# The quantised linear layer (F2) set into the last head of the third attention layer (L2)

## The reference, cut to what matters

```python
x = x + tanh(g_xattn[2]) * L2_xattn(layernorm(x), ctx, Wq, Wk, Wv, Wo)   # 32 query heads of 128, 4 key/value heads
x = x + tanh(g_ffn[2]) * L2_ffn(layernorm(x), kernel, bias)
# L2_ffn: xq = fake_quant(x, 8 bit, per row); kq = fake_quant(kernel, 8 bit, per column)
#         y = xq @ kq + fake_quant(bias, 16 bit);  out = fake_quant(y, 8 bit, per row)
```

## Time and profile before

| | us |
|---|---|
| median of 3 runs | 1754.78 (1753.35 to 1755.42) |
| the profiled execution | 1753.51 |
| its span, first to last instruction | 1751.2 |
| granted TensorE clock over the span | 0.952 |
| PE busy | 1569.3 (90%) |
| DVE busy | 908.8 (52%) |
| ACT busy | 702.3 (40%) |
| POOL busy | 630.3 (36%) |

### The profile page before, as it was taken

One profiled execution on the slowest core, in us unless ns is written; L12 is line 12 of the kernel. 1 busy time (PEld: TensorE's weight loads), 2 busy tenths in 40 slices (PEclk: granted clock), 3 DMA queues, 4 the chain that ended last, 5 costly groups with the idle time before them and its releaser, 6 DMA issues. The chain is left out here.

```text
span 1751.2 us, 25554 instructions
## 1 busy us (share of the span) xinstructions
PE 1569.3 (90%) x8786; PEld 1236.8 (71%) x8786; DVE 908.8 (52%) x1777; ACT 702.3 (40%) x2015; POOL 630.3 (36%) x594
## 2 busy tenths in 40 slices
PE   5897979858889999999999998686899999999976
PEld 4565756547668888888888887565677777777752
DVE  4785558867531212221222223596776676667552
ACT  3442154344335444443543534452333333343321
POOL 3543145466223221331331312133644444444310
PEclk9998999978989999999999999896999999999996
DMA  5001010011221010110101000332212121211001
GB/s 199 1 1 48 25 42 13 1 65 59 67 67 48 13 49 1 61 49 2 49 5 44 25 25 1 126 73 73 73 49 73 49 85 43 79 49 49 13 16 48
DMA packets 27885, 81.41 MB, mean 46 GB/s; under 512 B 3248, under 2 KB 11952, under 8 KB 22768
## 3 DMA queue, kind: packets, MB, share of 16 engines
q1 hardware_dynamic: 26896, 79.44, 13.8%
q10 hardware_dynamic: 864, 0.30, 0.1%
HBM read 69.25 MB, written 10.49 MB: 46 GB/s over the span
## 5 line engine op out<-in xcount | busy, mean ns | idle before, releaser
L385 PE MATMUL bank<-hid_high,wq_high 128*128 128x512 f32 (+1 forms) x640 | 257.6, 403 | 6.8 <-issue 6.5
L385 PE MATMUL bank<-hid_high,wq_low 128*128 128x512 f32 (+1 forms) x640 | 239.5, 374 | 0.0
L385 PE MATMUL bank<-hid_low,wq_high 128*128 128x512 f32 (+1 forms) x640 | 238.1, 372 | 0.0
L1132 DVE SCALAR_TENSOR_TENSOR x_stream<-bank,gates,x_stream 128x512 f32<-128x512 f32 x64 | 48.1, 751 | 364.8 <-PE bank L1218 364.8
L982 POOL TENSOR_TENSOR probs_middle<-probs_middle,small 128x512 f32<-128x512 f32 x64 | 66.5, 1040 | 365.1 <-DVE small L1120 365.1
L1468 ACT ACTIVATE probs_last<-probs_last,small 128x64 f32<-128x64 f32 x256 | 86.0, 337 | 154.3 <-DVE small L1540 154.3
L385 PEld LDWEIGHTS bank<-hid_high,wq_high 128*128 128x128 f32 x640 | 122.4, 191 | 30.8 <-issue 9.8
L385 PEld LDWEIGHTS bank<-hid_high,wq_low 128*128 128x128 f32 x640 | 122.1, 191 | 23.0
L385 PEld LDWEIGHTS bank<-hid_low,wq_high 128*128 128x128 f32 x640 | 122.8, 192 | 21.0 <-issue 3.5
L1052 ACT ACTIVATE probs_middle<-pair,small 128x128 f32<-128x128 f32 x256 | 90.5, 366 | 75.5 <-DVE small L1114 75.5
L583 POOL TENSOR_TENSOR probs_first<-probs_first,small 128x512 f32<-128x512 f32 x64 | 66.7, 1043 | 134.2 <-DVE small L737 134.1
(11 more groups left out here) (277 smaller groups left out, 4010.5 us busy)
## 6 DMA issues: line engine op xcount, KB each, us to landing
raw_q<-in_L_wq SPq DMA_DIRECT2D x18, 1024.0 KB, 4.9
raw_o<-in_L_wo SPq DMA_DIRECT2D x18, 1024.0 KB, 4.8
values_last<-ctx_values SPq DMA_DIRECT2D x32, 256.0 KB, 3.9
values_t_last<-ctx_keys SPq DMA_DIRECT2D x8, 512.0 KB, 3.3
raw_c<-in_L_wkv SPq DMA_DIRECT2D x6, 512.0 KB, 3.7
x_stream<-in_x SPq DMA_DIRECT2D x8, 256.0 KB, 9.5
ctx_keys<-raw_o SPq DMA_DIRECT2D x8, 256.0 KB, 2.0
ctx_values<-raw_o SPq DMA_DIRECT2D x16, 128.0 KB, 2.4
```

The costliest lines, as they stand in the source:

```text
L385: last = k.nc.tensor.matmul(out, stationary(a, c), moving(b, c), start=n == 0, stop=n == total - 1)
L1132: nc.vector.scalar_tensor_tensor(xt, k.bank[7][:], gate, xt, ALU.mult, ALU.add).then_inc(k.x_done, 1)
```

## The change

F2 has no stage of its own. Its work is handed out by `linear_gpsimd`, `linear_scalar`, `linear_vector`, `linear_tensor` and called from attention_middle's last head. `F2_AT` is 13: linear step f stands in slot 13+f, so steps 0 to 5 run in slots 13 to 18, the rest behind the slots.
- Weights: greatest values on DVE at the end of slot 6, rounding on ACT at the end of slot 7, clipping on DVE at the end of slot 8, transposes on PE at the end of slots 11 and 12, evictions on ACT at the start of slots 12 and 13, the scales matmul at the end of PE's slot 13.
- The rounded weights are put in `raw_c`, where the bias goes too: its DMA waits for the scales matmul, and `fake_bias` follows in DVE's step 0.
- The rows of statistics are now taken for one tile at a time (`tile_stats`, then a power on POOL).
- On PE, transposes_x(t) stands in slot 15+t ahead of the attention's transposes and project; linear(t) at the slot's end. Both products use one bank each (4 and 5) instead of two.
- The sixteen context groups all stand behind the slots, four in each of tiles 4 to 7. The first unit's weights are split by ACT after its step 5 and by POOL ahead of its step 6.
- L3's first weights are fetched earlier. The scratch buffers are allocated once; L2's second query buffer is made of halves of `values_t` and `probs_t`.

```diff
@@ attention_middle, ACT @@
                 for s in range(SLOTS + (LAG if last else 0)):
+                    if last and s in (12, 13):
+                        integer_weights(2 * s - 24)
+                        integer_weights(2 * s - 23)
+                    if last and s == 14:
+                        weight_scales()
                     if lives(first, last, s):
                         exp(j, s)
+                    if last and s >= F2_AT + 2:
+                        integers(s - F2_AT - 2)
...
+                    if last and s == 7:
+                        round_weights(k.at("loaded_q", 32 * HEADS + 16))
+                    if last and s >= F2_AT:
+                        linear_step(s - F2_AT)
             heads(act, body)
+            for f in range(SLOTS + LAG - F2_AT, LIN_STEPS):
+                t = f - 2
+                if t < T:
+                    integers(t)
+                linear_step(f)
+                if t == 3:
+                    context_weights(0)
+                if 4 <= t < T:
+                    for g in range(4 * t, 4 * t + 4):
+                        context_evict(g)
+                if t == 4:
+                    context_weights(1)
@@ attention_middle, DVE @@
                     if lives(first, last, s - LAG):
                         out_low(j, s - LAG)
+                    if last and s == 6:
+                        weight_scales(k.at("loaded_q", 32 * HEADS + 16))
+                    if last and s == 8:
+                        clip_weights()
+                    if last and s == F2_AT - 1:
+                        tile_stats(0, updated + 1)
+                    if last and s >= F2_AT:
+                        linear_step(s - F2_AT, updated)
@@ attention_middle, PE @@
                     if lives(first, last, s):
                         scores(j, s)
+                    if last and s >= F2_AT + 2:
+                        transposes_x(s - F2_AT - 2)
...
                     if lives(first, last, s - LAG):
                         attend(j, s - LAG)
+                    if last and s in (11, 12):
+                        pe.wait_ge(k.q_sbuf, tile("q_sbuf", j, SLOTS))
+                        integer_weights(2 * s - 22)
+                        integer_weights(2 * s - 21)
+                    if last and s == 13:
+                        weight_scales()
+                    if last and s >= F2_AT + 2:
+                        linear(s - F2_AT - 2)
             heads(pe, body)
+            pe.wait_ge(k.exp_done, k.at("exp_done", SLOTS * HEADS))
+            for t in range(SLOTS + LAG_Y - F2_AT - 2, T):
+                transposes_x(t)
+                context_group(4 * t)
+                context_group(4 * t + 1)
+                linear(t)
+                context_group(4 * t + 2)
+                context_group(4 * t + 3)
@@ attention_middle, POOL @@
+                    if last and s >= F2_AT - 1:
+                        linear_step(s - F2_AT)
...
+            for f in range(SLOTS + LAG_Y - F2_AT, LIN_STEPS):
+                if f in (SLOTS + LAG_Y - F2_AT, SLOTS + LAG_Y - F2_AT + 1):
+                    context_weights(f - SLOTS - LAG_Y + F2_AT)
+                linear_step(f)
@@ linear_sync @@
+    fetch_ahead(k, sp, "L3", "q", k.wround_done, k.at("wround_done", C))
+    fetch_ahead(k, sp, "L3", "o", k.lo_o, used_o)
+    sp.wait_ge(k.wint_psum, k.at("wint_psum", C))
+    sp.wait_ge(k.scales_psum, k.at("scales_psum", 1))
+    sp.dma_start(m["bias"], k.args["F2_bias"].partition_broadcast(P)).then_inc(k.loaded_const, 16)
+    sp.wait_ge(k.s_psum, scores_done)
+    ctx_fetch(k, sp, 2, m["RAW"][0])
+    sp.wait_ge(k.o_psum, attend_done)
+    ctx_fetch(k, sp, 3, m["RAW"][1])
@@ linear_gpsimd, step(f) @@
+        if 0 <= f + 1 < T:
+            rstd(f + 1)
+        if 2 <= f < T + 2:
+            add_bias(f - 2)
@@ linear_scalar, step(f) @@
+        if f >= 4:
+            integers_y(f - 4)
+        if 1 <= f <= T:
+            round_x(f - 1)
+        if 3 <= f < T + 3:
+            round_y(f - 3)
@@ linear_vector, step(f, updated): order of the calls @@
+        normalise(f); fake_bias() at f == 0
+        greatest(f - 1); greatest_y(f - 3); scale, zero_to_one, inverse of both
+        update(f - 4); gated_scale(f - 3); tile_stats(f + 1, updated + f + 2)
+        clip(f - 1); clip_y(f - 3); next_stats(f - 5); scaled_y(f - 2)
```

More of the change, by code:

```diff
@@ L155, in __init__ @@
         self.values_dram = nc.dram_tensor("ctx_values", (8, S, B * P), F32, kind="Internal").ap()
[L157 to L167, removed]
     def at(self, name, n):
@@ L987, in _ @@
                 low_q(0, 0, head)
+            linear_step, context_weights = linear_gpsimd(k, pool)
             def body(j, first, last):
-                for s in range(SLOTS):
+                for s in range(SLOTS + (LAG_Y if last else 0)):
                     u, t = divmod(s, T)
@@ L1242, in _ @@
                 queries(0, g)
+            integer_weights, weight_scales, transposes_x, linear, context_group = linear_tensor(k, pe)
             def body(j, first, last):
@@ new lines, in linear_buffers @@
+    return dict(
+        wt=k.raw_q, wint=[k.vt[:, 0:D], k.vt[:, D:2 * D], k.raw_c[:, 0:D], k.raw_c[:, D:2 * D]],
+        ks=k.raw_c[:, 0:D], bias=k.raw_c[:, D:2 * D], diag=k.e[:, 4 * D:5 * D],
+        XS=ring(k.q[:, 0:2 * D], D), QX=ring(k.q[:, 2 * D:4 * D], D), QT=ring(k.wc[0], D), Y=ring(k.vt[:, 0:2 * D], D),
+        QY=ring(k.kt[:, 0:2 * D], D), sc=[k.small[:, 176 + 8 * i:184 + 8 * i] for i in range(4)],
+        sw=k.small[:, 208:212], iw=k.small[:, 212:216], sb=k.small[:, 216:218],
+        RAW=[[k.vt[:, 1024:2048], k.pt[:, 1024:2048]], [k.vj[:, 0:1024], k.vj[:, 1024:2048]]])
@@ new lines, in linear_tensor, with weights, scales, transposes @@
+def linear_tensor(k, pe):
+    nc, m = k.nc, linear_buffers(k)
+    def weights(c):
+        pe.wait_ge(k.wclip_done, k.at("wclip_done", C))
+        if c >= 2:
+            pe.wait_ge(k.wint_sbuf, k.at("wint_sbuf", c - 1))
+        for f in range(C):
+            last = nc.tensor.transpose(k.bank[4 + c % 2][:, f * P:(f + 1) * P], m["wint"][f][:, c * P:(c + 1) * P],
+                                       k.ident[:])
+        last.then_inc(k.wint_psum, 1)
+    def scales():
+        pe.wait_ge(k.diag_ready, k.at("diag_ready", 1))
+        pe.wait_ge(k.wint_sbuf, k.at("wint_sbuf", C - 1))
+        nc.tensor.matmul(k.bank[4][:], k.ones[:], m["diag"], start=True, stop=True).then_inc(k.scales_psum, 1)
+    def transposes(t):
+        pe.wait_ge(k.clip_done, k.at("clip_done", t + 1))
+        if t:
+            pe.wait_ge(k.int_sbuf, k.at("int_sbuf", t))
+        else:
+            pe.wait_ge(k.scales_sbuf, k.at("scales_sbuf", 1))
+        for c in range(C):
+            last = nc.tensor.transpose(k.bank[4][:, c * P:(c + 1) * P], m["QX"][t % 2][:, c * P:(c + 1) * P], k.ident[:])
+        last.then_inc(k.int_psum, 1)
+    def linear(t):
+        pe.wait_ge(k.int_sbuf, k.at("int_sbuf", t + 1))
+        if t == 0:
+            pe.wait_ge(k.wint_sbuf, k.at("wint_sbuf", C))
+        else:
+            pe.wait_ge(k.y_scaled, k.at("y_scaled", t))
+        for c in range(C):
+            last = nc.tensor.matmul(k.bank[5][:], m["QT"][t % 2][:, c * P:(c + 1) * P], k.wq[0][:, c * D:(c + 1) * D],
+                                    start=c == 0, stop=c == C - 1)
+        last.then_inc(k.lin_psum, 1)
+    def group(g):
+        ctx_product_tensor(k, pe, g, k.bank[g % 2][:])
+    return weights, scales, transposes, linear, group
```

507 lines of the change are left out of this document (231 added, 276 removed).

## The result

The changed kernel takes 1771.97 us (median of 4 runs, 1771.41 to 1774.28), the kernel before 1754.40 in the same rounds (4 runs, 1753.35 to 1755.42). The ratio is 1.0103, with a 95% interval of 1.0090 to 1.0116. It is slower, by 17.6 us; 1772 was predicted. The profiled execution took 1771.41 us, with a span of 1769.3 and a mean granted clock of 0.947.

A forecast was written before the change was run, and what follows sets the result against it. PE, busy 90% of the span, was taken as the bound, with time to win only where it idles. 1753.5 + 7.3 (change at full clock) + 10 (lost clock) = 1770.8 us; median 1.3 higher, so 1772, range 1757 to 1785.

The forecast's parts named there:

- slot 15: L2's last head: transposes_x, transposes, project and attend about 6.0 us, then DVE's step to the clip: 9.0, cold burst +1.9.
- end of step 5, add_bias, split: Ahead of group 16: rest of step 5 1.9 us, POOL's bias 1.4, then its split of the first unit 5.4.
- sixteen groups: Context groups behind the slots, four per tile in four tiles: 48.9 us without stalls between, plus 1.9 for the clock.
- tail: After the groups: evictions, integers_y 1.2 us, round_y to F2's last update 3.6; 4.9 us in all.
- The ring and PE's queue: Slots 13 to 18: DVE's step lengthens the maximum-to-out_low loop; PE's transposes_x wait for clips; 56.7 us at full clock, 31.2 before.
- The bias: Slot 13: DVE waits 2.2 us for the late bias DMA, then fake_bias takes 2.5, its 512-wide operations 0.42 each.
- The wait for the split: Ahead of group 16: PE waits about 8 us for POOL's low parts of the first context weights.
- The clock: Half-rate starts after PE's idle: +1.9 us in four slots, 0.6 in slot 14, 1.9 at the groups; +10, bounds 0 and 21.
- The weights: Slots 6 to 12: F2's weight work among the attention slots delays maximum(13) by 2.7 us, bounds 1 and 6.
- the ring is not lengthened: Rival: slots 13 to 18 cost only DVE's work, 41.4 us, clock stays up; -9.9 us, 1745; chance 0.10.
- The clock holds: Rival: PE's bursts in the slots are enough to keep the full clock; +7.3 us, 1762; chance 0.18.
- It comes out even: Rival: shorter weights and DMA, no lost clock, steps 1 to 5 each 1 us shorter; +1 us, 1756; chance 0.05.

The follow-up runs named there:

- e3: Changed kernel plus 114 extra matmuls, results unread, in PE's idle time in slots 14 and 16 to 18 and ahead of group 16; 1763.44 us.
- e1: Changed kernel with PE's transposes of x and ACT's integers of a tile moved behind attend and out_high of their slot; 1757.44 us.
- e2: Changed kernel with the first context weights loaded early into the raw query buffer and split in slots 13 and 14; 1762.92 us.
- e5: Changed kernel with the bias loaded early into raw_o, and L3's first output weights fetched at F2's end; 1770.92 us.
- e4: Changed kernel with eight tiles behind slot 18, two context groups in each of the first seven, fake_bias and first unit's split in slots 16 and 17; 1744.24 us.

## Why the prediction was right

| step | predicted us | measured us |
|---|---|---|
| weights in slots 6 to 12 | +2.7 | +3.1 |
| slot 13 | 11.0 | 11.5 |
| slot 14 | 8.3 + 0.6 | 9.0 |
| slot 15 | 9.0 + 1.9 | 9.1 |
| slot 16 | 9.7 + 1.9 | 12.6 |
| slot 17 | 10.3 + 1.9 | 12.1 |
| slot 18 | 8.35 + 1.9 | 11.1 |
| end of step 5, add_bias, split | 1.9 + 1.4 + 5.4 | 9.1 |
| sixteen groups | 48.9 + 1.9 | 51.3 |
| tail | 4.9 | 4.4 |

The second number of a predicted sum is the clock's.

- **The ring and PE's queue**: right, in mechanism and size. e3 shows its length at full clock to 0.3 us in slots 16 to 18, e1 that the order of PE's queue, with ACT's beside it, makes it so.
- **The bias**: the wait was 2.17 us for 2.2. The three 512-wide operations took 0.48, 0.43 and 0.48 us beside a silent POOL, for 0.42 each; the earlier trace rows has 1.52 beside add_bias. By the rule on the shared port (the Trainium skill, Advanced Engine Details and Errata, "VectorE Performance Modes") they had to be short, and the trace agrees.
- **The wait for the split**: 8.29 us for about 8; e2 takes it out.
- **The clock**: 10 us forecast; e3 returned 7.5 net and 10.1 without slot 15, which was cold there and not in the kernel after. By the rule of the Trainium skill (TensorE: Matmul & The Clock Gate, "What's actually happening") this term had to be there, and the trace agrees: the clock fell to 0.50 with each of the waits of 3.43 to 8.29 us, though not always at once (the transposes after 3.43 us took 1.12 us, those after 4.14 us 0.89, those after 4.35 us still 0.63). Its place was off: slot 15 was not cold, though the same burst was cold in e2 and e5, while slots 16 and 18 lost 2.8 and 2.4 in place of 1.9 (12.6 and 11.1 against 9.8 and 8.6 in e3), and the groups 2.85 (5.7 us at half rate). That these errors cancel is luck: the six slots were forecast at 64.9 with the clock's 8.2, and took 65.4, but a cold slot 15 alone would have added 1.6 to 2.6 (e5, e2 and e3). The half-rate burst was priced by one row; how much of a burst runs cold differs from one to the next.
- **The weights**: 0.4 us short, of which slots 11 and 12 account for 0.55 (1.55 for 1.0 us). The bound taken from the nearest rows held it.
- **The rivals**: "the ring is not lengthened" asked for slots 13 to 18 under 51 us; they took 65.4. "The clock holds" falls by the table of stretches. "It comes out even" asked for steps 1 to 5 each 1 us shorter, and none was.

That no wait stood between the groups, and that the stages far away kept their time, came as predicted too.

## What to carry to other kernels

Before work is woven into a pipeline whose engines wait for each other in a ring, read where the ring's slack lies: idle time inside the ring is not free to work behind it, and an instruction that waits on another engine, placed ahead of the ring's next step in an in-order queue, costs its whole wait in every round. The same matmuls behind the attend (and ACT's step that waits for them) gave 16.5 us back, the clock's share in it included, and the statistics ahead of out_low instead of behind it 0.7 us in slot 14, 0.4 over all slots. Work that can stand beside a full engine (DVE's tile steps beside the context groups) is badly placed where that engine has to wait for it: with the eight tiles behind the slots and the first unit split earlier (e4) the time from maximum(13) on is 28.5 us shorter than in the kernel after.

## What of the hardware was not expected

A cold burst has no fixed price, and the same burst need not be cold in the next execution. Slot 15's begins 20.72 us after maximum(13) in the kernel after and in e2_rawq, with PE's work over the 80 us ahead of it the same to 0.01 us; its transposes took 0.66 us in one and 1.11 in the other, the slot 9.1 and 11.4. Within the kernel after, four bursts of like make lost nothing, 2.8, 1.6 and 2.4 us (slots 15 to 18; the last three against e3, the first against the prediction's 9.0 at full clock), by where the clock's return fell in them. So a saving of 2 us ahead of such a burst (e5, 2.2 us in slot 13, 0.5 in the whole) can't be judged by one pair of traces, and the clock can cost 1.5 us in a stage that no edit touched (the end of L3).
